# A blockwise attention stage: packed copies for queries and keys, and the causal mask of the maximum pass moved to TensorE

## The chip, the cores and the metric

The kernel runs on one core of a Trainium2 chip. The metric is the device time of one execution in microseconds (us), the median of several runs; lower is better.

## The reference

The program is six residual blocks over x of 4 x 1024 x 128: expert FFN, attention, expert FFN (layer 0), then expert FFN, gated attention, expert FFN (layer 1). Only the first attention is touched by the change. With 16 heads of 8 dimensions it computes, for a layer-normed x:

```python
qkv = x @ w_in.T + b_in
q, k, v = to_heads(split(qkv))              # 4 x 16 x 1024 x 8
scores = einsum('bhqd,bhkd->bhqk', q * (1 / sqrt(8)), k)
scores = scores + where(tril, 0, -inf)      # causal
attn = softmax(scores)
out = einsum('bhqk,bhkd->bhqd', attn, v) @ w_out.T + b_out
```

The FFN blocks before and after and the gated attention are the same in both kernels.

## The kernel before

`phase_attention` (line 643) works in 16 sections, n = 0 to 15: four batches of 1024 tokens, and four groups of four heads in each. `order()` (line 675) gives each piece of work a due time in units of one section, and `walk` lets every engine go through its pieces in that one order. The engines are tied together by semaphores, and each engine does its pieces strictly in that order.

**Projection** (`proj`, twice per w, once per half of 512 tokens). TensorE leaves q (w = 0) or k (w = 1) in a bank; ScalarE writes a rounded high part into `high` (line 980), VectorE the rest into `low` (line 1102). A product then needs three terms: high by high, low by high and high by low.

**Copies on the Sync queue.** `queries(n)` fills slot n % 3 of `q_st`: three DMAs of 32 partitions by 1024 (high, low, high; line 1056) and one DMA of eight rows of `k_pad` that sets the rows for the maxima (line 1058). `keys(n, h)` fills half h of slot n % 2 of `k_pad`: for each of four heads, three DMAs of 8 partitions by 512 (high, high, low; line 1070), so twelve. `k_pad` is zero outside the rows of its own head. `keys(n, h)` first waits (line 1065) until section n-2 is scored up to unit 8 (h = 0) or to its end (h = 1), since it writes over its slot.

**Maximum pass** (`max`, due from n-1.26 to n-0.30). For each of four heads, nine banks (`MAXB`) hold the scores of all 8 query tiles against the keys that they can see: 12 products a head, line 886. Before the first product of a section TensorE waits for its queries and the first half of its keys. VectorE takes the maximum of each bank (`peak`, lines 1109 to 1118): a block that touches the diagonal by a `tensor_tensor_reduce` that adds the tile `mask` (line 1114), each other block by a `tensor_reduce` (line 1116). The three banks of the ring `SMALL` are shared with transposes and projections. `neg` combines the maxima (lines 1123 to 1130, due n-0.3), `maxt` (due n-0.25) transposes them on TensorE (line 895), ScalarE copies them out (line 986), and Sync puts them into `q_st` (line 1045), so that the products of the next pass come out with the maximum taken off.

**Score and value passes** (due n to n+1). Twelve units in a section, for each two pairs of heads: TensorE scores (line 905), ScalarE takes the exponential (line 994), GpSimd clears the part above the diagonal (line 1028), TensorE multiplies by the values (line 924, fp32), due two units later. `oevac` and `ot` (lines 1001, 933) follow at the end of a half.

The due times put these pieces in this order on TensorE around the start of the maximum pass of section n+1 (with the section that they belong to): score (n-1, unit 7, pair 1), max (n, last), score (n-1, 8, 0), pv (n-1, 6), max (n+1, first), maxt (n), score (n-1, 8, 1).

Of the kernel before, what the change touches and what calls it, by code (L numbers as in the profile page):

```python
# [6 lines left out]
F32 = mybir.dt.float32  # L7
# [6 lines left out]
P = 128  # L14
# [628 lines left out]
def phase_attention(nc, k, a):  # L643
# [25 lines left out]
    def order():  # L669
# [13 lines left out]
        for n in range(SECTIONS):  # L683
# [43 lines left out]
    with ExitStack() as ctx:  # L727
# [8 lines left out]
        b_in, bo, ones = sb("b_in", [P, 3]), sb("bo", [P, D]), sb("ones", [2, S])  # L736
        mask = sb("mask", [P, G])
        st, mv, veps, rstd = sb("st", [P, NB, 6]), sb("mv", [P, NB, 2]), sb("veps", [P, NB]), sb("rstd", [P, NB])
        xn = sb("xn", [P, NB, D])
        xn_h, xn_l = sb("xn_h", [P, S], F32R), sb("xn_l", [P, S], F32R)  # L740
        high, low = sb("high", [P, 2, S], F32R), sb("low", [P, 2, S], F32R)
        q_st, k_pad = sb("q_st", [P, 3, S], F32R), sb("k_pad", [P, 2, HG, S], F32R)
        v_t, v_aug = sb("v_t", [P, S]), sb("v_aug", [P, 2, NB, H * VH + 32 - VH])
        mx, nm, mst = sb("mx", [P, HG, HALF * NB]), sb("nm", [P, HG * NB]), sb("mst", [P, 2 * HG * NB])
# [11 lines left out]
        with nc.Block() as block:  # L756
            @block.sync
            def _(sp):
# [7 lines left out]
                for p in range(2):  # L766
                    for j in range(HG):
                        rows = slice(MROW + j, MROW + j + HG + 1, HG)
                        sp.dma_start(k_pad[rows, p, j, :].bitcast(F32), ones[:]).then_inc(ones_in, 16)
# [11 lines left out]
            def _(pool):  # L781
                pool.memset(ones[:], 1.0)
# [13 lines left out]
            def _(dve):  # L796
                dve.memset(q_st[:].bitcast(F32), 0.0)
                dve.memset(mask[:, 0:G - P], 0.0)
                dve.tensor_copy(mask[:, G - P:G], k.const("causal"))
# [9 lines left out]
        xh_done, qk_high = sem("xh_done"), sem("qk_high")  # L809
# [34 lines left out]
        def _(pe):  # L844
# [31 lines left out]
            def peak(n, j, i):  # L876
                bank, full = fill(pe, "max", n, j, i)
                at = 0
                if i == 0 and j == 0:
                    pe.wait_ge(q_in[n % 3], 16 * 4 * (n // 3 + 1))  # L880
                    pe.wait_ge(k_in[n % 2][0], 16 * 3 * HG * (n // 2 + 1))
                if i == HALF1 and j == 0:
                    pe.wait_ge(k_in[n % 2][1], 16 * 3 * HG * (n // 2 + 1))
# [71 lines left out]
        def _(act):  # L955
# [16 lines left out]
            def proj(b, w, h):  # L972
                bank, _ = content(act, "proj", b, w, h)
                cut = slice(h * G, (h + 1) * G)
                if b > 0 and w == 0:
                    for p in range(3):
                        act.wait_ge(q_in[p], 16 * 4 * len(range(p, HG * b, 3)))
# [716 lines left out]
```

## Time and profile before

| what | value |
|---|---|
| median of 3 runs | 2221.54 us (2219.11 to 2221.6) |
| the profiled execution | 2220.21 us |
| its span, first to last instruction | 2218.5 us |
| TensorE busy | 1768.8 us, 80% |
| VectorE busy | 1464.7 us, 66% |
| ScalarE busy | 960.4 us, 43% |
| GpSimd busy | 706.0 us, 32% |
| mean granted TensorE clock | 0.903 |

The attention lies between 262 and 1022 us of the span. A share of the whole span is a mean over six phases; what the change can do has to be read inside that stretch. Each line of a profile names the source line (L886), the engine (PE is TensorE, PEld its weight loads, DVE VectorE, ACT ScalarE, POOL GpSimd, SPq the Sync queue's DMA issues), the tiles written and read, and what ended an idle time before the instruction.

### The profile page before, as it was taken

The page shows a single profiled execution, that of the slowest core. Times are in us where ns is not written, and L with a number is a line of the kernel's source. Part 1 is how long each engine was busy: PE and PEld are TensorE (multiplying, and loading weights), DVE is VectorE, ACT ScalarE, POOL GpSimd, SP SyncE. Part 2 cuts the span into 40 slices and gives each one's busy share as a digit, 9 for nine tenths or more (in the row PEclk, how much of TensorE's full clock was granted, in tenths as well). Part 3 has the DMA queues.
Part 4 walks back from the last instruction along what each step waited for, and adds up shares of the span by engine and source line. Part 5 has one row for each costly group of instructions (what it writes and reads, how often), then busy time and mean ns, then how long its engine had stood idle before and what let it go on. Part 6 is the DMA issues. An engine that isn't in the chain of part 4 may idle for free. (4 is left out here: it accounts for less than half of the span.)

```text
span 2218.5 us, 28736 instructions
## 1 busy us (share of the span) xinstructions
PE 1768.8 (80%) x8768; PEld 1267.4 (57%) x8768; DVE 1464.7 (66%) x4307; ACT 960.4 (43%) x1579; POOL 706.0 (32%) x641
## 2 busy tenths in 40 slices
PE   4988668787888688886888769999925666899997
PEld 3666434444444344543666557777824555677776
DVE  4788657665667566753878557767637775677774
ACT  2444314454455355554444335545512222455554
POOL 1444511201211211111444325555511110455554
PEclk8999858998999889997999979999967888999998
DMA  3000011100010001100000110000010000000001
GB/s 85 1 1 0 8 27 20 24 17 19 18 24 18 19 17 22 21 9 0 1 1 0 35 33 1 1 1 0 1 31 1 0 0 1 1 1 1 0 0 38
DMA packets 27250, 27.75 MB, mean 13 GB/s; under 512 B 9609, under 2 KB 19682, under 8 KB 27122
## 3 DMA queue, kind: packets, MB, share of 16 engines
q1 hardware_dynamic: 24418, 24.09, 4.8%
q10 hardware_dynamic: 2576, 2.10, 0.3%
q8 instruction: 58, 0.95, 0.2%
q14 instruction: 70, 0.57, 0.1%
q0 software_dynamic: 128, 0.03, 0.1%
HBM read 10.41 MB, written 2.10 MB: 6 GB/s over the span
## 5 line engine op out<-in xcount | busy, mean ns | idle before, releaser
L994 ACT ACTIVATE att_probs<-banks 128x1024 f32<-128x1024 f32 (+3 forms) x384 | 303.7, 812 | 200.9 <-PE banks L905 198.5
L886 PE MATMUL banks<-att_k_pad,att_q_st 128*128 128x512 f32 (+3 forms) x768 | 254.7, 418 | 135.7 <-DMA att_k_pad<-att_low 121.5
L1114 DVE CUSTOM_DVE_ANT_0 banks<-banks,att_mask 128x128 f32<-128x128 f32 (+3 forms) x512 | 235.7, 522 | 174.9 <-PE banks L886 174.4
L886 PEld LDWEIGHTS banks<-att_k_pad,att_q_st 128*128 128x128 f32 x768 | 139.0, 207 | 262.4 <-issue 206.6
L1028 POOL TENSOR_SCALAR_AFFINE_SELECT att_probs<-att_probs 128x512 f32<-128x512 f32 x128 | 81.6, 637 | 563.8 <-ACT att_probs L994 563.8
L905 PE MATMUL banks<-att_q_st,att_k_pad 128*128 128x512 f32 (+3 forms) x768 | 218.0, 369 | 0.6 <-ACT att_probs L994 0.4
L462 POOL TENSOR_TENSOR ffn1a_hid_l<-ffn1a_hid,ffn1a_hid_h 128x512 fp32r<-128x512 f32 x128 | 165.2, 1293 | 130.8 <-ACT ffn1a_hid_h L418 130.8
L462 POOL TENSOR_TENSOR ffn1b_hid_l<-ffn1b_hid,ffn1b_hid_h 128x512 fp32r<-128x512 f32 x128 | 165.3, 1294 | 129.3 <-ACT ffn1b_hid_h L418 129.3
L1116 DVE TENSOR_REDUCE att_mx<-banks 128x1 f32<-128x512 f32 x256 | 161.5, 683 | 36.0 <-PE banks L886 35.8
L924 PE MATMUL banks<-att_probs,att_v_aug 128*32 128x512 f32 (+3 forms) x1536 | 172.2, 521 | 0.6 <-POOL att_probs L1028 0.5
L905 PEld LDWEIGHTS banks<-att_q_st,att_k_pad 128*128 128x128 f32 x768 | 143.0, 200 | 39.1 <-ACT att_probs L994 20.0
L601 DVE TENSOR_TENSOR ffn1a_scl<-ffn1a_sil,banks 128x512 f32<-128x512 f32 x128 | 88.0, 687 | 84.3 <-PE banks L317 42.4
L601 DVE TENSOR_TENSOR ffn1b_scl<-ffn1b_sil,banks 128x512 f32<-128x512 f32 x128 | 88.0, 688 | 81.3 <-PE banks L317 40.7
L410 ACT ACTIVATE ffn1a_sil<-banks 128x512 f32<-128x512 f32 x128 | 76.7, 599 | 115.2 <-PE banks L312 112.4
L410 ACT ACTIVATE ffn1b_sil<-banks 128x512 f32<-128x512 f32 x128 | 76.7, 599 | 114.3 <-PE banks L312 111.5
L462 POOL TENSOR_TENSOR ffn0b_hid_l<-ffn0b_hid,ffn0b_hid_h 128x512 fp32r<-128x512 f32 x72 | 92.4, 1288 | 103.3 <-ACT ffn0b_hid_h L418 103.3
L462 POOL TENSOR_TENSOR ffn0a_hid_l<-ffn0a_hid,ffn0a_hid_h 128x512 fp32r<-128x512 f32 x72 | 92.4, 1287 | 102.9 <-ACT ffn0a_hid_h L418 102.9
L609 DVE TENSOR_TENSOR ffn1a_hid<-ffn1a_scl,banks 128x512 f32<-128x512 f32 x128 | 87.9, 687 | 7.6 <-POOL ffn1a_hid_l L462 2.4
L609 DVE TENSOR_TENSOR ffn1b_hid<-ffn1b_scl,banks 128x512 f32<-128x512 f32 x128 | 87.9, 687 | 6.3 <-POOL ffn1b_hid_l L462 1.8
L418 ACT ACTIVATE ffn1a_hid_h<-ffn1a_hid 128x512 fp32r<-128x512 f32 x128 | 79.9, 624 | 8.0 <-DVE ffn1a_hid L609 8.0
L418 ACT ACTIVATE ffn1b_hid_h<-ffn1b_hid 128x512 fp32r<-128x512 f32 x128 | 79.8, 624 | 4.5 <-DVE ffn1b_hid L609 4.5
L601 DVE TENSOR_TENSOR ffn0b_scl<-ffn0b_sil,banks 128x512 f32<-128x512 f32 x72 | 49.3, 685 | 40.8 <-PE banks L322 39.9
(439 smaller groups left out, 4302.4 us busy)
## 6 DMA issues: line engine op xcount, KB each, us to landing
att_q_st<-att_high SPq DMA_DIRECT2D x32, 128.0 KB
att_k_pad<-att_high SPq DMA_DIRECT2D x256, 16.0 KB
att_q_st<-att_low SPq DMA_DIRECT2D x16, 128.0 KB
att_k_pad<-att_low SPq DMA_DIRECT2D x128, 16.0 KB
out_dram<-x SPq DMA_DIRECT2D x1, 2048.0 KB, 8.7
raw<-in_L_ffn_w_dram SPq DMA_DIRECT2D x3, 512.0 KB, 13.7
raw<-in_L_ffn_w_down_dram SPq DMA_DIRECT2D x1, 1024.0 KB, 11.4
sel_raw<-in_consts_dram SPq DMA_DIRECT2D x1, 576.0 KB, 4.4
```

Source lines behind the costliest of these rows:

```text
L410: act.activation(sil[:, n, :], gate_ps[:, n, :], ACT.Silu).then_inc(silu_done, 1)
L418: act.activation(hid_h[:, n, :], hid[:, n, :], ACT.Copy).then_inc(high_cut, 1)
L462: pool.tensor_tensor(hid_l[:, n, :], hid[:, n, :], hid_h[:, n, :].bitcast(F32), ALU.subtract)\
L601: dve.tensor_tensor(scl[:, n, :], sil[:, n, :], comb_ps[:, comb_bank(q, c), :], ALU.mult).then_inc(scaled, 1)
L609: dve.tensor_tensor(hid[:, n, :], scl[:, n, :], up_ps[:, n, :], ALU.mult).then_inc(hidden, 1)
L886: mm = pe.matmul(bank[:, at:at + width], q_st[:, n % 3, t * P:(t + 1) * P], k_pad[:, n % 2, j, c * G:c * G + width], start=True, stop=True ...
L905: mm = pe.matmul(score_ps[:, pair, h, 0:c], k_pad[:, n % 2, 2 * pair + h, kb * P:(kb + 1) * P], q_st[:, n % 3, (qg + 1) * G - c:(qg + 1) * ...
L924: mm = pe.matmul(o_ps[32 * j:32 * j + 32, G - c:G], v_aug[:, b % 2, kb, at:at + 32], probs[:, unit % NPROB, j, 0:c], start=kb == 0, stop=k ...
L994: act.activation(probs[:, unit % NPROB, 2 * pair:2 * pair + 2, 0:c], score_ps[:, pair, :, 0:c], ACT.Exp, scale=SCALE).then_inc(exped, 1)
L1028: pool.affine_select(now, now, pattern=[[0, HG], [1, P]], base=0, channel_multiplier=-1, compare_op=ALU.is_ge, fill=0.0).then_inc(masked, 1)
L1114: ins = dve.tensor_tensor_reduce(now, now, mask[:, G - width:G], 1.0, -3e38, ALU.add, ALU.max, best)
L1116: ins = dve.tensor_reduce(best, now, AX.X, ALU.max)
```

## The change

1. `high` and `low` become one tile `parts` of 128 x 2 x 3 x 1024. Part 0 is the high part (ScalarE), one further part is the low part (VectorE, `LOW`), and the third is a copy of the high part (`AGAIN`), made by GpSimd in a new piece `proj`: a `tensor_copy` of 128 x 512 for each projection, 16 in all. A semaphore `qk_again` tells Sync of it.
2. `queries(n)` issues one DMA of 32 partitions by three rows into 96 partitions, and the one for the maxima rows as before: two in place of four. `keys(n, h)` issues one DMA a head, 8 partitions by three rows into 24 partitions: four in place of twelve. The rows of `q_st` and `k_pad` change places accordingly.
3. The diagonal blocks are masked on TensorE: after the product of such a block a second one, the identity by the causal tile, both bfloat16 and 128 columns wide, adds the mask into the last 128 columns. There are 8 such blocks a head and section, 512 in all.
4. VectorE reads each bank with one `tensor_reduce` (36 a section; four groups of 128, two of 256 or one of 512) into a wider `mx`, and `neg` reads this with another pattern.
5. The maximum pass is due from n-1.22 to n-0.29 in place of n-1.26 to n-0.30. With this `maxt(n)` and score (n-1, 8, 1) come before the first product of section n+1.
6. The tile `ones` lies in `xn`, the tile `mask` is gone, and `ident_b` and `causal_b` are made at the start of the phase.

```diff
+    LOW, AGAIN = (1, 2), (2, 1)
+    MAXTO = (slice(20, 21), slice(8, 9), slice(25, 26), slice(15, 16), slice(28, 29), slice(3, 7),
+             slice(29, 30), slice(11, 15), slice(16, 25, 8))
+    PARTS = (1, 1, 1, 1, 1, 4, 1, 4, 2)
...
-                    put(n - 1.26 + 0.96 * (i * HG + j) / (len(MAXB) * HG), "max", n, j, i)
+                    put(n - 1.22 + 0.93 * (i * HG + j) / (len(MAXB) * HG), "max", n, j, i)
...
-                    pe.wait_ge(q_in[n % 3], 16 * 4 * (n // 3 + 1))
-                    pe.wait_ge(k_in[n % 2][0], 16 * 3 * HG * (n // 2 + 1))
+                    pe.wait_ge(q_in[n % 3], 16 * 2 * (n // 3 + 1))
+                    pe.wait_ge(k_in[n % 2][0], 16 * HG * (n // 2 + 1))
...
+                    diag = c == t // TG
                     mm = pe.matmul(bank[:, at:at + width], q_st[:, n % 3, t * P:(t + 1) * P],
-                                   k_pad[:, n % 2, j, c * G:c * G + width], start=True, stop=True,
+                                   k_pad[:, n % 2, j, c * G:c * G + width], start=True, stop=not diag,
                                    skip_group_check=True)
                     at += width
+                    if diag:
+                        mm = pe.matmul(bank[:, at - P:at], ident_b[:], causal_b[:], start=False, stop=True,
+                                       skip_group_check=True)
...
+            def proj(b, w, h):
+                step = 4 * b + 2 * w + h
+                cut = slice(h * G, (h + 1) * G)
+                pool.wait_ge(qk_high, step + 1)
+                pool.tensor_copy(parts[:, w, AGAIN[w], cut], parts[:, w, 0, cut].bitcast(F32)).then_inc(qk_again, 1)
...
+                sp.wait_ge(qk_again, 4 * b + 2)
...
-                for r, part in enumerate((high, low, high)):
-                    sp.dma_start(q_st[32 * r:32 * r + 32, n % 3, :].bitcast(F32), part[own, 0, :].bitcast(F32))\
-                      .then_inc(q_in[n % 3], 16)
+                sp.dma_start(q_st[0:MROW, n % 3, :].bitcast(F32), parts[hg * 32:hg * 32 + 32, 0, :, :].bitcast(F32))\
                   .then_inc(q_in[n % 3], 16)
...
+                sp.wait_ge(qk_again, 4 * b + 3 + h)
                 for j in range(HG):
                     own = slice((hg * HG + j) * DH, (hg * HG + j) * DH + DH)
-                    for r, part in enumerate((high, high, low)):
-                        sp.dma_start(k_pad[32 * r + j * DH:32 * r + (j + 1) * DH, n % 2, j, cut].bitcast(F32),
-                                     part[own, 1, cut].bitcast(F32)).then_inc(k_in[n % 2][h], 16)
+                    sp.dma_start(k_pad[3 * DH * j:3 * DH * (j + 1), n % 2, j, cut].bitcast(F32),
+                                 parts[own, 1, :, cut].bitcast(F32)).then_inc(k_in[n % 2][h], 16)
...
-                for t, c in MAXB[i]:
-                    width = width_of(t, c)
-                    now, best = bank[:, at:at + width], mx[:, j, 2 * t + c:2 * t + c + 1]
-                    if c == t // TG:
-                        ins = dve.tensor_tensor_reduce(now, now, mask[:, G - width:G], 1.0, -3e38, ALU.add, ALU.max, best)
-                    else:
-                        ins = dve.tensor_reduce(best, now, AX.X, ALU.max)
-                    at += width
-                ins.then_inc(empty, 1)
+                dve.tensor_reduce(mx[:, j, MAXTO[i]], bank.rearrange("p (n c) -> p n c", n=PARTS[i]), AX.X, ALU.max)\
+                   .then_inc(empty, 1)
```

## Rows read from the trace of the kernel before

**Rows 1.** The page: busy time of each engine over the span.

```profile
PE 1768.8 (80%) x8768; PEld 1267.4 (57%) x8768; DVE 1464.7 (66%) x4307; ACT 960.4 (43%) x1579; POOL 706.0 (32%) x641
```

**Rows 2.** Busy time by stretch: stretch, length, engines (instructions), clock, DMA share, GB/s.

```profile
344.00:1016.00 672.00, 542.79 (x3299) 309.37 (x3298) 420.47 (x1380) 338.08 (x463) 111.60 (x160) 0.91 0.09 19
```

**Rows 3.** Who waited for whom, 300 to 1035 us: total, times, longest.

```profile
PE banks L886 <- DMA att_k_pad<-att_low: 121.5, 15, 10.8
PEld banks L886 <- DVE att_mx L1114: 27.9, 64, 2.9
PE banks L886 <- DVE att_mx L1114: 9.1, 10, 2.5
```

**Rows 4.** Timeline around one such wait: start, us, engine, line, operation, idle before.

```profile
584.59 0.63 PE L905 MATMUL banks<-att_q_st,att_k_pad 128*128 128x512 f32 x2
...
585.30 1.31 SPq L1070 DMA_DIRECT2D att_k_pad<-att_high  x2
...
585.85 1.07 PE L924 MATMUL banks<-att_probs,att_v_aug 128*32 128x512 f32 x8
...
592.65 0.62 SPq L1070 DMA_DIRECT2D att_k_pad<-att_low  x1
...
594.76 0.77 PE L886 MATMUL banks<-att_k_pad,att_q_st 128*128 128x512 f32 x1 [7.84 <-DMA att_k_pad<-att_low]
```

**Rows 5.** Timeline: the first and the last of the 14 such waits.

```profile
370.39 0.77 PE L886 MATMUL banks<-att_k_pad,att_q_st 128*128 128x512 f32 x1 [7.84 <-DMA att_k_pad<-att_low]
...
952.74 0.77 PE L886 MATMUL banks<-att_k_pad,att_q_st 128*128 128x512 f32 x1 [7.84 <-DMA att_k_pad<-att_low]
```

**Rows 6.** DMA issues by source line: count, ns min/median/max, first and last start.

```profile
L1070 SPq DMA_DIRECT2D att_k_pad<-att_low x128: 624/625/642, 300.4 to 969.9; - x128
L1056 SPq DMA_DIRECT2D att_q_st<-att_low x16: 584/591/602, 297.1 to 930.3; - x16
L142 SPq DMA_DIRECT2D raw<-in_L_ffn_w_dram x2: 433/560/686, 1.7 to 2.8; - x2
```

**Rows 7.** Timeline of the last section, where no keys are awaited.

```profile
986.98 0.27 PE L895 MATMUL banks<-pack,att_mst 128*64 128x128 f32 x1 [1.23 <-DVE att_mst L1130]
```

**Rows 8.** Busy time by stretch, right after two of the waits (columns as Rows 2).

```profile
594.70:598.40 3.70, 3.64 (x12) 2.44 (x16) 2.10 (x6) 1.51 (x3) 0.64 (x1) 0.50 0.03 9
598.40:602.10 3.70, 3.70 (x25) 1.72 (x18) 1.97 (x6) 1.90 (x3) 0.64 (x1) 0.99 0.00 0
644.40:649.60 5.20, 5.09 (x16) 2.42 (x16) 2.16 (x6) 2.11 (x3) 0.64 (x1) 0.50 0.04 11
```

**Rows 9.** Timeline: products in a row on TensorE.

```profile
566.94 0.33 PE L905 MATMUL banks<-att_q_st,att_k_pad 128*128 128x128 f32 x2
567.99 0.66 PE L933 MATMUL banks<-pack,att_o_sb 128*128 128x128 f32 x4
```

**Rows 10.** Groups of instructions by form, 300 to 1035 us: busy, mean ns, idle before.

```profile
L886 PE MATMUL banks<-att_k_pad,att_q_st 128*128 128x128 f32 x128 | 36.0, 281 | 8.6 <-DVE att_mx L1114 7.5 <-DVE att_low L1102 0.6
```

**Rows 11.** Groups of instructions on the page: busy, mean ns, idle before.

```profile
L1114 DVE CUSTOM_DVE_ANT_0 banks<-banks,att_mask 128x128 f32<-128x128 f32 (+3 forms) x512 | 235.7, 522 | 174.9 <-PE banks L886 174.4
L1028 POOL TENSOR_SCALAR_AFFINE_SELECT att_probs<-att_probs 128x512 f32<-128x512 f32 x128 | 81.6, 637 | 563.8 <-ACT att_probs L994 563.8
L462 POOL TENSOR_TENSOR ffn1a_hid_l<-ffn1a_hid,ffn1a_hid_h 128x512 fp32r<-128x512 f32 x128 | 165.2, 1293 | 130.8 <-ACT ffn1a_hid_h L418 130.8
L1116 DVE TENSOR_REDUCE att_mx<-banks 128x1 f32<-128x512 f32 x256 | 161.5, 683 | 36.0 <-PE banks L886 35.8
```

**Rows 12.** Timeline of the phase's start.

```profile
294.85 2.09 ACT L980 ACTIVATE att_high<-banks,att_b_in 128x512 fp32r<-128x512 f32 x3 [0.59 <-PE banks L858]
...
296.49 0.56 SPq L1056 DMA_DIRECT2D att_q_st<-att_high  x1
...
299.08 1.32 SPq L1070 DMA_DIRECT2D att_k_pad<-att_high  x2
...
308.55 1.62 PE L886 MATMUL banks<-att_k_pad,att_q_st 128*128 128x512 f32 x3 [10.75 <-DMA att_k_pad<-att_low]
```

More of the change, by code:

```diff
@@ L735, in phase_attention @@
         wo_t = sb("wo_t", [P, P])
-        b_in, bo, ones = sb("b_in", [P, 3]), sb("bo", [P, D]), sb("ones", [2, S])
-        mask = sb("mask", [P, G])
+        b_in, bo = sb("b_in", [P, 3]), sb("bo", [P, D])
+        ident_b, causal_b = sb("ident_b", [P, P], BF16), sb("causal_b", [P, P], BF16)
         st, mv, veps, rstd = sb("st", [P, NB, 6]), sb("mv", [P, NB, 2]), sb("veps", [P, NB]), sb("rstd", [P, NB])
         xn = sb("xn", [P, NB, D])
+        ones = xn[0:2, :, :].rearrange("p t d -> p (t d)")
         xn_h, xn_l = sb("xn_h", [P, S], F32R), sb("xn_l", [P, S], F32R)
-        high, low = sb("high", [P, 2, S], F32R), sb("low", [P, 2, S], F32R)
+        parts = sb("parts", [P, 2, 3, S], F32R)
         q_st, k_pad = sb("q_st", [P, 3, S], F32R), sb("k_pad", [P, 2, HG, S], F32R)
         v_t, v_aug = sb("v_t", [P, S]), sb("v_aug", [P, 2, NB, H * VH + 32 - VH])
-        mx, nm, mst = sb("mx", [P, HG, HALF * NB]), sb("nm", [P, HG * NB]), sb("mst", [P, 2 * HG * NB])
+        mx, nm, mst = sb("mx", [P, HG, 4 * NB]), sb("nm", [P, HG * NB]), sb("mst", [P, 2 * HG * NB])
         m_t = sb("m_t", [2 * HG * NB, P])
@@ L768, in _ @@
                         rows = slice(MROW + j, MROW + j + HG + 1, HG)
-                        sp.dma_start(k_pad[rows, p, j, :].bitcast(F32), ones[:]).then_inc(ones_in, 16)
+                        sp.dma_start(k_pad[rows, p, j, :].bitcast(F32), ones).then_inc(ones_in, 16)
                 sp.wait_ge(w_in, 16 * 6)
@@ L781, in _ @@
             def _(pool):
-                pool.memset(ones[:], 1.0)
+                pool.memset(ones, 1.0)
                 pool.memset(k_pad[:].bitcast(F32), 0.0).then_inc(zeroed, 1)
@@ L797, in _ @@
                 dve.memset(q_st[:].bitcast(F32), 0.0)
-                dve.memset(mask[:, 0:G - P], 0.0)
-                dve.tensor_copy(mask[:, G - P:G], k.const("causal"))
+                dve.tensor_copy(ident_b[:], k.ident)
+                dve.tensor_copy(causal_b[:], k.const("causal"))
                 dve.wait_ge(high_done, 1)
@@ L976, in proj @@
                     for p in range(3):
-                        act.wait_ge(q_in[p], 16 * 4 * len(range(p, HG * b, 3)))
+                        act.wait_ge(q_in[p], 16 * 2 * len(range(p, HG * b, 3)))
                     for p in range(2):
-                        act.wait_ge(k_in[p][h], 16 * 3 * HG * (HG * b // 2))
-                act.activation(high[:, w, cut], bank, ACT.Identity, bias=b_in[:, w:w + 1]).then_inc(qk_high, 1)
+                        act.wait_ge(k_in[p][h], 16 * HG * (HG * b // 2))
+                act.activation(parts[:, w, 0, cut], bank, ACT.Identity, bias=b_in[:, w:w + 1]).then_inc(qk_high, 1)
             def maxt(n):
@@ L1035, in wo @@
                 pool.tensor_tensor(xs, xs, ypos[:].rearrange("p t d -> p (t d)"), ALU.add).then_inc(x_added, 1)
-            walk(dict(norm=norm, mask=mask, wo=wo))
+            walk(dict(norm=norm, proj=proj, mask=mask, wo=wo))
         @block.sync
@@ L1101, in proj @@
                 dve.wait_ge(qk_high, 4 * b + 2 * w + h + 1)
-                dve.scalar_tensor_tensor(low[:, w, cut], bank, b_in[:, w:w + 1], high[:, w, cut].bitcast(F32),
+                dve.scalar_tensor_tensor(parts[:, w, LOW[w], cut], bank, b_in[:, w:w + 1], parts[:, w, 0, cut].bitcast(F32),
                                          ALU.add, ALU.subtract).then_inc(empty, 1)
@@ L1122, in neg @@
                     drained(dve, "max", n, j, len(MAXB) - 1)
-                dve.tensor_reduce(nm[:], mx[:].rearrange("p j (t c) -> p (j t) c", c=HALF), AX.X, ALU.max, negate=True)\
+                dve.tensor_reduce(nm[:].rearrange("p (j q o) -> p j o q", q=NB // 2, o=2),
+                                  mx[:].rearrange("p j (o q s) -> p j o q s", o=2, s=4), AX.X, ALU.max, negate=True)\
                    .then_inc(neg_steps, 1)
```

9 lines of the change are left out of this document (4 added, 5 removed).

## The prediction

> **What bounds the kernel now.** I read the page first, only to see that no engine is full over the whole span [rows 1]; six phases are mixed there. So I took the stretch from the first score to near the last, 344 to 1016 us [rows 2]. TensorE is busy 542.8 of its 672 us, VectorE 420.5, ScalarE 338.1. Then the list of waits in the phase [rows 3]. TensorE waits for the keys' DMAs 15 times, 121.5 us in all; the next entries, waits of its weight loads and products for VectorE, come to 37.0 us together (27.9 + 9.1). One of the 15 is the start (10.75 us, [rows 12]), the other 14 lie one in each section from n = 2 on, the first and the last 7.84 us long [rows 5] and the rest no shorter (121.5 - 10.75 = 110.75 for all 14); 14 x 7.84 = 109.8 us is what I count. Without these, 672 - 109.8 = 562 us are left, and TensorE is busy in 543 of them, 97%. (A busy time with waiting weight loads in it says too much, but nothing else is near.) So in the attention TensorE sets the pace, and its largest hole is the wait for keys.
>
> The timeline shows why the hole is there [rows 4]. The score product that starts at 584.59 frees the slot, and Sync issues the first key DMA at 585.30. Twelve follow, the last at 592.65: (592.65 - 585.30) / 11 = 0.668 us apart. The last has landed 2.1 us after its issue, at 594.76. TensorE is through with its value products at 585.85 + 1.07 = 586.92 and stands until 594.76. Landing is thus 9.46 us after the first issue, of which 7.35 us are the issuing of eleven further DMAs.
>
> **Part 1, key DMAs: four in place of twelve.** The last issue is 3 x 0.668 = 2.0 us after the first. An issue takes 0.62 us for 8 rows of 2 KB and 0.59 us for 32 rows of 4 KB [rows 6], so it doesn't go by rows; a three-dimensional load of 1024 rows of 512 B was issued in 0.43 to 0.69 us. I take 0.67. Each DMA now carries three times the bytes, for which I add 0.5 us (an estimate: twelve DMAs of one row an engine moved inside 0.67 us intervals, so three rows can't need more than 2 us, and the DMA engines are 9% busy here [rows 2]). Landing: 2.0 + 2.1 + 0.5 = 4.6 us after the first issue, 589.9 on the clock of [rows 4]; bounds 4.1 and 6.1.
>
> The Trainium skill, "DMA: Bandwidth & Descriptors", section "Why a DMA increments its semaphore by 16 and not by 1", says that the number of DMA engines is the largest up to 16 that divides the slowest dimension of both sides; 8 and 24 partitions would give eight engines as before, three rows on each. By that the packing wins issue time but no width, and the 0.5 us are needed; with 16 engines they would be about half, 14 x 0.25 = 3.5 us less in the sum.
>
> **Part 2, the new order.** Between the freeing of the slot and the first product of the new section TensorE now has one more bank of the section before (about 0.5 us with its mask products), `maxt` (0.3 to 0.4) and one more score pair (0.63 less overlap, 0.45). `maxt` waits for VectorE to finish the maxima and for `neg`. Today that is hidden behind the keys, but the last section, which awaits no keys, shows it: 1.23 us [rows 7]. So TensorE would come to the keys at 586.92 + 0.5 + 1.23 + 0.4 + 0.45 = 589.5, against 589.9: 0.4 us left. New waits: 1.23 + 0.4 = 1.7 us in a section, 14 x 1.7 = **24 us back of 109.8** (bounds 1.2 and 3.5 us a section). Everything on TensorE is queued behind the wait at `maxt`: the scores, and with them ScalarE, which has slack.
>
> **Part 3, the clock.** After each wait the granted clock is 0.50, that is 1.2 GHz, for 3.7 to 5.2 us, and then 0.99, 2.4 GHz [rows 8]. In that time TensorE does 12 products in 3.7 us against 25 in the next 3.7 (not the same mix). Before it, TensorE had done nothing for 7.84 us. With waits of 1.2 and 0.4 us I expect most drops to vanish; half of 4.4 us is 2.2, of which I take 1.5 since not all of that stretch is bound by TensorE: **-21 us** (bounds 0 and -29). The Trainium skill, "TensorE: Matmul & The Clock Gate", section "HAM oscillation — how this bites in real kernels", also describes waits for DMA that bring the clock down each time; the trace agrees with 0.50 behind these waits, and whether 1.2 us of idling suffices no row here says.
>
> **Part 4, the start.** The first key DMA is issued at 299.08 and the first product starts at 308.55 [rows 12]. The query copies now also wait for two GpSimd copies of 128x512, not in the trace; GpSimd's nearest are 0.64 us (one operand, in place) and 1.29 us (two operands, fp32r out) [rows 11], I take 1. The second high part is ready at about 295.55 (294.85 plus a third of 2.09), so queries start at 296.6 rather than 296.49, two DMAs later keys start at 297.9, held by no copy (third copy about 297.4), and land at 302.5 to 303: **-5.6 us**. In the later batches the same copies are due 0.15 to 0.3 of a section ahead of the queries, and GpSimd is 17% busy (111.6 of 672, [rows 2]): nothing. Where it delays a mask by a copy of 1 us, the value products come two units later.
>
> **Part 5, 512 more products on TensorE.** None of them is in the trace. 32 of them belong to section 0, where VectorE's maxima set the pace alone; 480 lie on the bound engine. Lower bound: two 128-column products in a row end 0.33 us after the first starts, one alone takes 0.27, so the second adds 0.06 us [rows 9]. Upper, with each product behind a load: four in 0.66 us, (0.66 - 0.27) / 3 = 0.13 us. The load of the identity can go on under the 128 to 512 columns ahead of it, but the load that follows has only 128 columns to hide under. I take 0.09, between them: 480 x 0.09 = **+43 us** (29 to 62). The far end is a product whose whole 0.28 us are exposed [rows 10]; that is a rival below.
>
> The Trainium skill, "TensorE: Matmul & The Clock Gate", section "Back-to-back issue gap", gives N / 2.4 + 2.5 ns, 56 ns for 128 columns, and its section on fast weight load lets bfloat16 weights of 128 columns load faster than fp32. By that the sum of this part would be 27 us, at the lower bound from the rows; no run so far shows a bfloat16 load here.
>
> **Part 6, VectorE.** For one head and section it has 8 masked blocks at a mean of 0.522 us and 4 reductions at 0.683 [rows 11], 6.9 us, part of it overlapped; nine reductions of 512 columns are 9 x 0.683 = 6.1. It gets up to 0.8 us a head faster, 3 us a section, and it isn't the bound: 0, with up to -15 us if 15 of the 37.0 us of waits for it [rows 3] go. The new `neg` reads 128 x 128 in place of 128 x 64, about 0.1 us more in each chain; nothing. The two setup copies take the place of one memset and one copy: nothing.
>
> **Sum**, against the profiled 2220.2 us (1.3 us below the median of 2221.5): -109.8 + 24 - 21 - 5.6 + 43 = -69, so 2151 us.
>
> **The rivals.**
>
> - A, *the mask products cost next to nothing*, hidden in the gaps that the ring's waits leave anyway [rows 3], and VectorE's relief counts. For it: two 128-column products 0.06 us apart [rows 9]. Against: 97% busy. Saves 30 of the 43 and 10 of the waits: about 2111 us.
> - B, *a leftover wait keeps the clock down*: the keys land 1.5 us later than I say and each section still idles 3.2 us in pieces, with the clock at 0.50 behind it. 2151 + 14 x 1.5 + 21 = 2193 us. For it: three rows on each engine, and the wait at `maxt` is one that the old order hid.
> - C, on the other side, *the mask products drain the array*: a change from fp32r to bfloat16 and back lets each of the 480 be exposed with its full 0.28 us [rows 10], 134 us. The time is 2220.2 - 112.4 + 134 = 2242, slower. It decides from 112.4 / 480 = 0.234 us a product on. Against it: the products with fp32 weights and with fp32r weights follow each other in this trace without such a price ([rows 4], 584.59 to 585.85).
> - D, *the packing wins nothing*: a DMA's issue goes by its rows after all, 2 us for each, so that the keys land as late as now. What is gained is the 1.3 us of work moved ahead of the wait, 14 x 1.3 = 18, and 43 are paid: 2245 us, slower. Against: [rows 6].
>
> **How the numbers follow.** The forecast gets 0.55, A 0.20, B 0.15, C 0.07, D 0.03. The predicted time is 2151. Its own range is 2130 to 2175 by the bounds of parts 1, 3 and 5. To hold the time 8 times in 10 the range takes in A and B, 2108 to 2200; left out are C, D and the edges. About 0.2% (4.4 us) is what a measurement of this kernel can tell from no change. Faster by more than that are the forecast, A and B with 0.89, 0.02 is for between, slower are C and D with 0.09.
>
> **What would show it.** Part 1: four issues of about 0.65 us apart at the line of the keys, and a wait of under 1 us there in place of 7.84. Part 2: a wait of 1 to 1.5 us at `maxt` for `neg`, in every section. Part 3: the clock at 0.99 where `maxt` and the first maxima of a section run. Part 4: the first product of section 0 near 303 us. Part 5: starts of the bfloat16 product and the next one 0.06 to 0.13 us apart; the time from section to section down from 44.8 us ((952.74 - 370.39) / 13, [rows 5]) to some 40. What would make the prediction wrong is a price of the mask product outside 0.06 to 0.13, or an issue of a key DMA of over 1 us.

## The result and the profile after

The changed kernel takes 2141.85 us (median of 4 runs, 2139.88 to 2143.93), the one before 2220.32 beside it. The ratio is 0.9651, with a 95% interval of 0.9633 to 0.9668: 3.5% faster, 78 us. The profiled execution has a span of 2138.1 us against 2218.5, 80.4 less. All of it lies in the attention: from the first transposes of its weights to the last of its products it takes 944.99 - 269.73 = 675.3 us, and took 1022.56 - 266.70 = 755.9. (The phase starts 3 us later in this execution and the phases behind it are 3 us shorter; such shifts between executions bound what single profiles can tell.)

First who waits for whom in the changed kernel, from 300 to 950 us (total, times, longest), which answers [rows 3]. L892 is the product of the maximum pass, L897 its mask product, L904 the transpose of the maxima, L1123 the reduction, L1084 the key DMA.

```profile
PE banks L892 <- DMA att_k_pad<-att_parts: 27.5, 15, 5.6
PEld banks L892 <- DVE att_mx L1123: 16.5, 35, 1.7
PE banks L904 <- DVE att_mst L1137: 7.0, 16, 2.0
PE banks L892 <- DVE att_mx L1123: 2.2, 3, 0.8
```

The waits for keys are 27.5 us in place of 121.5: one of 5.6 at the start and 14 of some 1.56. The waits for VectorE at the banks fell from 45.7 us (37.0 behind the masked blocks, [rows 3], and 8.7 behind the plain reductions) to 18.7, and the transpose of the maxima waits 7.0 us in all, 2.0 of them in section 0.

The timeline around the same place as in [rows 4], one section of the changed kernel:

```profile
552.22 0.39 PE L914 MATMUL banks<-att_q_st,att_k_pad 128*128 128x512 f32 x1
...
552.68 2.84 SPq L1084 DMA_DIRECT2D att_k_pad<-att_parts  x4
...
553.99 1.07 PE L933 MATMUL banks<-att_probs,att_v_aug 128*32 128x512 f32 x8
...
555.39 0.27 PE L904 MATMUL banks<-pack,att_mst 128*64 128x128 f32 x1 [0.33 <-DVE att_mst L1137]
...
555.41 0.71 PE L914 MATMUL banks<-att_q_st,att_k_pad 128*128 128x512 f32 x2
...
557.61 0.47 PE L892 MATMUL banks<-att_k_pad,att_q_st 128*128 128x512 f32 x1 [1.48 <-DMA att_k_pad<-att_parts]
```

Four issues begin at 552.68 and end 2.84 us later, so with 0.67 us for one they follow each other every 0.72 us ((2.84 - 0.67) / 3). The keys are there at 557.61, 4.93 us after the first issue, where it was 9.46. TensorE now does the transpose and one more score pair before it asks for them.

The stretches, as in [rows 2] and [rows 8]: first the kernel before over 344 to 930 us, then the changed one over the same.

```profile
344.00:930.00 586.00, 466.68 (x2813) 270.08 (x2813) 379.02 (x1226) 284.59 (x392) 99.09 (x140) 0.90 0.10 20
```

```profile
344.00:930.00 586.00, 550.80 (x3698) 311.27 (x3694) 387.66 (x717) 332.58 (x450) 115.26 (x167) 0.99 0.12 21
```

TensorE is busy 94% of the time in place of 80%, and the granted clock went from 0.90 to 0.99. The issues and the two new kinds of instruction, as in [rows 6] and [rows 11] (count, ns min/median/max, first and last start; the last line is a group of the page):

```profile
L1084 SPq DMA_DIRECT2D att_k_pad<-att_parts x128: 670/673/1212, 300.7 to 885.4; - x128
L1037 POOL CAST att_parts<-att_parts x16: 609/612/617, 297.1 to 743.7; 128x512 fp32r<-128x512 f32 x16
L897 PEld LDWEIGHTS banks<-att_causal_b,att_ident_b x512: 94/96/149, 306.7 to 907.3; 128*128 128x128 bf16 x171
...
L1123 DVE TENSOR_REDUCE att_mx<-banks 128x1 f32<-128x512 f32 (+2 forms) x576 | 367.9, 685 | 146.8 <-PE banks L897 111.1
```

### The profile page after: what moved, and what is told of

It reads as the page before. It is cut to its first block and busy times, and to the rows that moved or that the text cites. A ratio compares the mean times of both kernels' runs of the same rounds, so it can differ in the third digit from the quotient of the medians.

```text
span 2138.1 us, 28801 instructions
## 1 busy us (share of the span) xinstructions
PE 1788.4 (84%) x9280; PEld 1275.3 (60%) x9280; DVE 1434.0 (67%) x3603; ACT 963.9 (45%) x1579; POOL 714.6 (33%) x657
## 5 line engine op out<-in xcount | busy, mean ns | idle before, releaser
L1123 DVE TENSOR_REDUCE att_mx<-banks 128x1 f32<-128x512 f32 (+2 forms) x576 | 367.9, 685 | 146.8 <-PE banks L897 111.1
L892 PE MATMUL banks<-att_k_pad,att_q_st 128*128 128x512 f32 (+3 forms) x768 | 268.9, 416 | 31.9 <-DMA att_k_pad<-att_parts 27.5
L892 PEld LDWEIGHTS banks<-att_k_pad,att_q_st 128*128 128x128 f32 x768 | 148.8, 200 | 128.7 <-issue 105.7
L933 PE MATMUL banks<-att_probs,att_v_aug 128*32 128x512 f32 (+3 forms) x1536 | 166.6, 506 | 0.6 <-POOL att_probs L1043 0.5
L914 PEld LDWEIGHTS banks<-att_q_st,att_k_pad 128*128 128x128 f32 x768 | 130.7, 193 | 22.0 <-ACT att_probs L1003 11.3
L897 PE MATMUL banks<-att_causal_b,att_ident_b 128*128 128x128 bf16 x512 | 118.2, 235 | 0.0
L897 PEld LDWEIGHTS banks<-att_causal_b,att_ident_b 128*128 128x128 bf16 x512 | 50.6, 99 | 47.3 <-issue 25.2
## 6 DMA issues: line engine op xcount, KB each, us to landing
raw<-in_L_ffn_w_dram SPq DMA_DIRECT2D x3, 512.0 KB, 13.7
```

Source lines behind the costliest of these rows:

```text
L897: mm = pe.matmul(bank[:, at - P:at], ident_b[:], causal_b[:], start=False, stop=True, skip_group_check=True)
L914: mm = pe.matmul(score_ps[:, pair, h, 0:c], k_pad[:, n % 2, 2 * pair + h, kb * P:(kb + 1) * P], q_st[:, n % 3, (qg + 1) * G - c:(qg + 1) * ...
L933: mm = pe.matmul(o_ps[32 * j:32 * j + 32, G - c:G], v_aug[:, b % 2, kb, at:at + 32], probs[:, unit % NPROB, j, 0:c], start=kb == 0, stop=k ...
L1123: dve.tensor_reduce(mx[:, j, MAXTO[i]], bank.rearrange("p (n c) -> p n c", n=PARTS[i]), AX.X, ALU.max)\
```

## The experiments

The change has three parts that can be taken one at a time: P, the packed DMAs; D, the new due times; M, the mask on TensorE with the single reduction on VectorE. My theory was that TensorE sets the pace, that P and D remove its wait, and that M costs it time. Each kernel was timed beside the kernel before; runs of different sets were on different chips, so I compare ratios. Times are medians in us. Multiplied by 2220 a ratio step of 0.001 is 2.2 us.

| parts | kernel | time | ratio (95% interval) |
|---|---|---|---|
| P | packed DMAs alone | 2152.5 | 0.9694 (0.9678 to 0.9711) |
| M | mask alone | 2245.4 | 1.0112 (1.0095 to 1.0129) |
| D | due times alone | 2211.0 | 0.9960 (0.9947 to 0.9972) |
| P M | changed kernel, old due times | 2175.3 | 0.9794 (0.9763 to 0.9824) |
| P D | changed kernel, mask on VectorE | 2113.2 | 0.9514 (0.9498 to 0.9530) |
| M D | changed kernel, twelve key DMAs | 2230.3 | 1.0054 (1.0037 to 1.0071) |
| P M D | the changed kernel | 2141.9 | 0.9651 (0.9633 to 0.9668) |

### The mask products left out

```diff
-                    if diag:
-                        mm = pe.matmul(bank[:, at - P:at], ident_b[:], causal_b[:], start=False, stop=True,
-                                       skip_group_check=True)
```

> The changed kernel with its 512 mask products left out: the maximum pass then takes maxima over the unmasked diagonal blocks (that part of the computation is changed). Everything else stays. Theory P (TensorE sets the pace, a mask product costs 0.09 us): 480 x 0.09 = 43 us less, of which some 4 come back because TensorE reaches the keys earlier: 2142 - 43 + 4 = 2103 us. Rival H (the mask products lie in gaps that are there anyway): within 5 us of 2142. Rival X (a bfloat16 product between fp32r ones costs its own 0.04 us and about 0.085 us of gap ahead of it, 0.125 in all): 2142 - 60 + 4 = 2086 us.

Measured: 2104.4 us, ratio 0.9472 (0.9452 to 0.9492). 37.5 us less by the medians, 39.7 by the ratios, so 0.078 to 0.083 us for each of 480 products. That is theory P's cost: the products are not hidden. Its 4 us that come back are not seen, though. Without the products TensorE waits less for the keys (23.4 us in place of 27.5) and more for the maxima (13.7 in place of 7.0) and for VectorE's banks (30.4 in place of 18.7), 14 us more in all. The 0.08 us is thus what is left after those waits: if they all count, the products themselves took up to (37.5 + 14) / 480 = 0.11 us each (an estimate from the two lists of waits), and a quarter of that lay in waits that are there anyway.

### Packed DMAs alone

The edit: from the changed kernel, the mask and the maxima on VectorE as before (its tile `mask` back, no mask products) and the due times set back.

```diff
-                    put(n - 1.22 + 0.93 * (i * HG + j) / (len(MAXB) * HG), "max", n, j, i)
+                    put(n - 1.26 + 0.96 * (i * HG + j) / (len(MAXB) * HG), "max", n, j, i)
...
-                    if diag:
-                        mm = pe.matmul(bank[:, at - P:at], ident_b[:], causal_b[:], start=False, stop=True,
...
+                    if c == t // TG:
+                        ins = dve.tensor_tensor_reduce(now, now, mask[:, G - width:G], 1.0, -3e38, ALU.add, ALU.max, best)
+                    else:
+                        ins = dve.tensor_reduce(best, now, AX.X, ALU.max)
```

> Packed DMAs alone: query and key copies as in the changed kernel, but the mask added by VectorE as before, the old due times (n-1.26 to n-0.30), no mask products. Theory P: the keys land 4.93 us after the first issue as measured in the changed kernel, TensorE reaches them 1.62 us after it as before, so the wait is 3.3 us in place of 7.84: 14 x 4.5 = 63 us less, 5 at the start, and 5 to 15 of the clock: 2220 - 63 - 5 - 10 = 2142 us, as fast as the full change. Rival V (VectorE's relief carries the gain, the DMAs little): above 2190 us.

Measured: 2152.5 us, 67 less than before, far from rival V but 10 more than I expected. Its wait line (300 us to the end of the phase) and its stretch over 344 to 930 us:

```profile
PE banks L892 <- DMA att_k_pad<-att_parts: 53.4, 15, 5.3
```

```profile
344.00:930.00 586.00, 520.01 (x3149) 296.98 (x3149) 415.50 (x1369) 320.99 (x438) 114.02 (x164) 0.94 0.12 21
```

The waits are what I said, (53.4 - 5.3) / 14 = 3.4 us each. What is missing is the 10 us of the clock: the waits shrank by 121.5 - 53.4 = 68.1 us and the span by 2218.5 - 2150.5 = 68.0, so next to nothing came back beside them. The mean clock is 0.94 in place of 0.90 all the same, because a mean over a stretch counts the waits themselves. In the kernel before, the clock falls while TensorE still waits (first line, behind its last product at 586.92); here it falls near the end of the wait or behind it, and the products pay as before (second line, right behind a wait of 3.31 us):

```profile
592.00:593.00 1.00, 0.00 (x0) 0.00 (x0) 0.00 (x0) 0.00 (x0) 0.00 (x0) 0.50 0.12 23
```

```profile
607.36:613.38 6.02, 6.02 (x18) 3.20 (x19) 2.23 (x7) 2.11 (x3) 0.64 (x1) 0.50 0.04 10
```

Added up from the clock and the products in the traces, from 344 us to the end of the attention, TensorE worked at 0.50 for 68.7 us in the kernel before, for 66.9 here, and for 13.7 in the changed kernel.

### The mask alone

The edit is that of the change (its items 3 and 4) in the kernel before, with twelve key DMAs and the old due times.

```diff
+                    if diag:
+                        mm = pe.matmul(bank[:, at - P:at], ident_b[:], causal_b[:], start=False, stop=True,
+                                       skip_group_check=True)
...
-                        ins = dve.tensor_tensor_reduce(now, now, mask[:, G - width:G], 1.0, -3e38, ALU.add, ALU.max, best)
+                dve.tensor_reduce(mx[:, j, MAXTO[i]], bank.rearrange("p (n c) -> p n c", n=PARTS[i]), AX.X, ALU.max)\
```

> The mask alone: the kernel before with the mask as bfloat16 products on TensorE and one reduction a bank on VectorE, old due times, twelve key DMAs. Theory P: 480 x 0.09 = 43 us more, 0 to 10 back from waits for VectorE: 2253 to 2263 us, slower than before. Rival V (VectorE's relief carries the gain): 2180 us or less. Rival X (0.125 us a product): 2270 to 2280 us.

Measured: 2245.4 us, 25 more than before. Rival V falls: relieving VectorE doesn't carry the gain. It is less than my 33 to 43 though; the waits of weight loads for VectorE's maxima, 36.6 us in the lists of the kernel before (27.9 of them in [rows 3]), are 14.6 here:

```profile
PEld banks L890 <- DVE att_mx L1116: 14.6, 35, 1.6
```

### The old due times under the full change

```diff
-                    put(n - 1.22 + 0.93 * (i * HG + j) / (len(MAXB) * HG), "max", n, j, i)
+                    put(n - 1.26 + 0.96 * (i * HG + j) / (len(MAXB) * HG), "max", n, j, i)
```

> The changed kernel with the old due times of the maximum pass (n-1.26 and 0.96). Theory P: TensorE reaches the keys about 1.5 us earlier (one bank, the transpose of the maxima and one score pair come behind the wait again), so the wait is 3.3 us in place of 1.5 and the wait for the maxima goes: 14 x 1.5 = 21 us more, and up to 15 if the clock drops behind a wait of 3.3 us: 2163 to 2178 us. Rival O (the order moves nothing, idle time only changes its place): within 4 us of 2142.

Measured: 2175.3 us, 33 more. Rival O falls. Its waits for keys are 50.0 us in place of 27.5, those for the maxima 1.8 in place of 7.0 and those for VectorE's banks 21.2 in place of 18.7: 20 us of the 35 by which the spans differ (2173.4 - 2138.1). The other 15 go with the clock, at 0.96 in place of 0.99 over 344 to 950 us; TensorE works at 0.50 for 43.8 us, not 13.7:

```profile
PE banks L892 <- DMA att_k_pad<-att_parts: 50.0, 15, 5.6
```

```profile
344.00:950.00 606.00, 552.06 (x3620) 314.65 (x3620) 387.35 (x714) 321.91 (x437) 113.65 (x163) 0.96 0.11 20
```

### Packed DMAs and new due times, mask on VectorE

The edit is that of the packed kernel above, without its first hunk.

> Packed DMAs and the new due times, but the mask added by VectorE as before: the changed kernel without its part on TensorE. Theory S (the parts add, VectorE isn't the bound): the packed kernel with old due times took 2152.5, and the new due times gave 2175.3 - 2141.9 = 33 us with the mask on TensorE, so 2119 us, faster than the full change; the kernel without any mask product and with the short reductions, 2104.4, is the floor. Rival D (the new due times need VectorE relieved: the transpose of the maxima now stands ahead of the keys and waits for VectorE's longer chain): the wait there grows to 2 us a section, 2140 us or more.

Measured: 2113.2 us, ratio 0.9514 (0.9498 to 0.9530). This is faster than the full change by 0.0137, 30 us. The waits of its phase:

```profile
PEld banks L892 <- DVE att_mx L1125: 36.1, 95, 2.0
PE banks L901 <- DVE att_mst L1141: 21.2, 16, 2.4
PE banks L892 <- DMA att_k_pad<-att_parts: 15.0, 15, 5.6
```

Rival D is right in its mechanism and wrong in its weight. Without the relief the transpose of the maxima does wait, 2.4 us in section 0 and 1.2 to 1.6 in each other one (21.2 over 16), but in that time the keys land, so their waits shrink from 27.5 to 15.0.

### Each mask product twice

```diff
                     if diag:
+                        pe.matmul(bank[:, at - P:at], ident_b[:], causal_b[:], start=False, stop=False,
+                                  skip_group_check=True)
                         mm = pe.matmul(bank[:, at - P:at], ident_b[:], causal_b[:], start=False, stop=True,
```

> The changed kernel with each mask product issued twice in a row (the mask is then added twice, which leaves masked places masked). Theory P (a mask product costs its columns wherever it stands; leaving 480 out saved 37.5 us, 0.078 each): 2142 + 37 = 2179 us. Rival L (what costs is the fp32r weight load that follows the 128 columns and can't hide under them, once for each pair): only the product itself is added, 0.04 to 0.06 us, 2161 to 2171 us. Rival H (hidden): 2142 us.

Measured: 2163.8 us, ratio 0.9735 (0.9719 to 0.9751): 22 us more for 480 products by the medians, 19 by the ratios, 0.04 to 0.05 each. The first one costs 0.08. That is the range of theory L. The timeline (L899 is the second of the two):

```profile
568.58 0.47 PE L892 MATMUL banks<-att_k_pad,att_q_st 128*128 128x512 f32 x1 [1.37 <-DMA att_k_pad<-att_parts]
568.89 0.23 PE L897 MATMUL banks<-att_causal_b,att_ident_b 128*128 128x128 bf16 x1
568.96 0.22 PE L899 MATMUL banks<-att_causal_b,att_ident_b 128*128 128x128 bf16 x1
```

The doubled product starts 0.07 us behind the first.

### The mask in fp32r

```diff
-        ident_b, causal_b = sb("ident_b", [P, P], BF16), sb("causal_b", [P, P], BF16)
+        ident_b, causal_b = sb("ident_b", [P, P], F32R), sb("causal_b", [P, P], F32R)
```

> The changed kernel with the identity and the causal tile in fp32r in place of bfloat16. Rival C of the prediction in its small form (it is the change of type that costs: the pair of a 256-column product and its mask product takes 0.246 us in the trace of the changed kernel, where two 256-column products alone are 0.117 apart): up to 0.04 us less for each of 480, 2122 us. Theory L (the cost is the next weight load, which hasn't enough columns to hide under): no change, 2137 to 2147 us, or up to 0.03 us more for each where the identity's own load is longer, 2157 us.

Measured: 2145.9 us, ratio 0.9658 (0.9642 to 0.9674), no difference from 0.9651. In the sum neither the change of type nor the bfloat16 decides, although the weight load of the identity is recorded at 191 ns here and at 96 in bfloat16:

```profile
L897 PEld LDWEIGHTS banks<-att_causal_b,att_ident_b x512: 187/191/338, 306.5 to 909.8; 128*128 128x128 f32 x171
```

But the equal times are a balance of two small differences. Behind a 256-column product, the product and its mask take 0.23 us in fp32r (the first lines) and 0.25 us in bfloat16 (the second):

```profile
554.50 0.33 PE L892 MATMUL banks<-att_k_pad,att_q_st 128*128 128x256 f32 x1
554.67 0.22 PE L897 MATMUL banks<-att_causal_b,att_ident_b 128*128 128x128 f32 x1
554.73 0.33 PE L892 MATMUL banks<-att_k_pad,att_q_st 128*128 128x256 f32 x1
```

```profile
552.61 0.36 PE L892 MATMUL banks<-att_k_pad,att_q_st 128*128 128x256 f32 x1
552.82 0.23 PE L897 MATMUL banks<-att_causal_b,att_ident_b 128*128 128x128 bf16 x1
552.86 0.36 PE L892 MATMUL banks<-att_k_pad,att_q_st 128*128 128x256 f32 x1
```

Behind a 128-column and a 384-column product, the two pairs together take 0.51 us in fp32r (551.48 to 551.99 in that trace) and 0.49 in bfloat16 (540.44 to 540.93). So rival C in its small form isn't excluded: what it would save at the wide products can be what the longer load of an fp32r identity costs at the narrow ones. No run separates the two.

### A semaphore for the first head's keys

```diff
+        k_first = [sem(f"k_first{p}") for p in range(2)]
...
-                    pe.wait_ge(k_in[n % 2][0], 16 * HG * (n // 2 + 1))
+                    pe.wait_ge(k_first[n % 2], 16 * (n // 2 + 1))
+                if i == 0 and j == 1:
+                    pe.wait_ge(k_in[n % 2][0], 16 * (HG - 1) * (n // 2 + 1))
...
-                                 parts[own, 1, :, cut].bitcast(F32)).then_inc(k_in[n % 2][h], 16)
+                                 parts[own, 1, :, cut].bitcast(F32)).then_inc(k_first[n % 2] if h == j == 0 else k_in[n % 2][h], 16)
```

> The changed kernel with a semaphore of its own for the first head's key DMA, so that TensorE waits for one DMA before the first product and for the other three only before the second head's. Theory P: the wait of 1.5 us goes and some 0.3 to 0.5 us come back one bank later: 14 x 1.1 = 15 us less, and the four short half clocks go: 2124 to 2130 us. Rival M (the wait moves whole to the second head): within 4 us of 2142.

Measured: 2130.5 us, ratio 0.9582 (0.9565 to 0.9599), but with runs from 2127.5 to 2140.1 us, of which the profiled one is the slowest. In its trace the waits only shrank from 27.5 to 22.9 us:

```profile
PE banks L895 <- DMA att_k_pad<-att_parts: 22.9, 16, 3.6
```

Each section still has a wait of 1.2 to 1.9 us, now one product later, so most of it goes to the second head, as rival M has it. The waits are 4.6 us shorter in this trace, yet its span is that of the changed kernel (2138.4 against 2138.1), so the phases outside made up for it in this execution. The medians show 11 us of gain and the ratios 15, which is theory P's number without its mechanism. Where the rest of the gain comes from stays open.

### The due times alone

```diff
-                    put(n - 1.26 + 0.96 * (i * HG + j) / (len(MAXB) * HG), "max", n, j, i)
+                    put(n - 1.22 + 0.93 * (i * HG + j) / (len(MAXB) * HG), "max", n, j, i)
```

> The kernel before with the new due times alone: twelve key DMAs, mask on VectorE. Theory P (the keys land 9.46 us after their first issue whatever TensorE does; the new order puts some 1.5 us of work, a wait for the maxima among it, ahead of that): 14 x 1.0 to 1.5 = 14 to 21 us less, 2200 to 2207 us. Rival A (the parts add as if independent: the new due times are worth 33 to 39 us anywhere): 2181 to 2187 us. Rival O (nothing until the keys are quick): 2220 us.

Measured: 2211.0 us, 9 less than before; the interval (0.9947 to 0.9972) leaves no doubt of a small gain, less than theory P's 14 to 21. The waits for keys fall by 38 us, but 18.4 come back at the transpose of the maxima (21.2 in place of 2.8 in the sections without keys, [rows 7]), and 8 more at the banks that VectorE frees (53.6 us in place of 45.7; the second line is their largest part, 27.9 in [rows 3]). That leaves 12 us by the waits, and the spans differ by 9.4:

```profile
PE banks L886 <- DMA att_k_pad<-att_low: 83.6, 15, 10.8
...
PEld banks L886 <- DVE att_mx L1114: 36.2, 95, 2.0
...
PE banks L895 <- DVE att_mst L1130: 21.2, 16, 2.4
```

Rival A falls: the due times are worth 9 us with slow keys and 40 us with quick ones (0.9694 against 0.9514).

### Twelve key DMAs under the full change

```diff
-                    sp.dma_start(k_pad[3 * DH * j:3 * DH * (j + 1), n % 2, j, cut].bitcast(F32),
-                                 parts[own, 1, :, cut].bitcast(F32)).then_inc(k_in[n % 2][h], 16)
+                    for r in range(3):
+                        sp.dma_start(k_pad[3 * DH * j + r:3 * DH * (j + 1):3, n % 2, j, cut].bitcast(F32),
+                                     parts[own, 1, r, cut].bitcast(F32)).then_inc(k_in[n % 2][h], 16)
```

The counts that TensorE and ScalarE wait for are three times as large.

> The changed kernel with its key copies issued as twelve DMAs again, into the new rows; queries packed, mask on TensorE, new due times. Theory P: the keys land at about 9.3 us after the first issue in place of 4.93, so each of 14 waits is 4.4 us longer, 62 us, and the clock falls behind each, 10 to 20 us: 2214 to 2224 us. Rival Q (part of the gain comes from the packed queries or from the smaller load on the Sync queue elsewhere): 2190 us or less.

Measured: 2230.3 us, ratio 1.0054 (1.0037 to 1.0071). It is slower than the kernel before, and 6 us above theory P's range; packing the keys is worth 88 us here. This pair also measures the clock, since both have the same products in the same order. The twelve-DMA kernel's waits and its stretch:

```profile
PE banks L892 <- DMA att_k_pad<-att_parts: 94.2, 15, 10.1
```

```profile
330.00:980.00 650.00, 550.64 (x3488) 309.26 (x3487) 388.03 (x714) 312.27 (x423) 111.01 (x160) 0.91 0.10 20
```

The spans differ by 2225.1 - 2138.1 = 87.0 us, the waits for keys by 94.2 - 27.5 = 66.7. The waits for the maxima and for VectorE's banks are the same within 1 us. The other 20.3 us go with a clock of 0.91 in place of 0.99: TensorE works at 0.50 for 69.6 us in place of 13.7.

### Two kernels on top of the faster combination

Packed DMAs, new due times, mask on VectorE and the first head's semaphore; then the same with the maximum pass due later:

```diff
-                    put(n - 1.22 + 0.93 * (i * HG + j) / (len(MAXB) * HG), "max", n, j, i)
+                    put(n - 1.19 + 0.90 * (i * HG + j) / (len(MAXB) * HG), "max", n, j, i)
```

> Packed DMAs, new due times, mask on VectorE, and the semaphore of its own for the first head's keys. Theory P: the kernel without that semaphore took 2113.2 and its trace has 9.4 us of waits for keys behind the start, most of which go: 2104 to 2110 us. Rival M (the wait only goes to the second head or to the transpose of the maxima): 2110 to 2116 us.

Measured: 2110.2 us, ratio 0.9504 (0.9489 to 0.9520), not told apart from the 0.9514 without the semaphore; it lies at the edge of both theories. The waits for keys are 11.1 us in place of 15.0.

> As the kernel with packed DMAs, new due times, mask on VectorE and the first head's semaphore, but the maximum pass due from n-1.19 over 0.90. Theory P (the remaining waits are keys that are a little late): the last of them go, 2100 to 2108 us. Rival D (the maxima end no earlier, so the wait at the transpose of the maxima stays, and a denser pass makes TensorE wait for VectorE's reductions more): equal to or slower than the kernel with n-1.22 and 0.93.

Measured: 2105.9 us, ratio 0.9482 (0.9466 to 0.9498). It is the fastest kernel here that does the whole computation, 1.7% below the changed kernel; its step from 0.9504 is inside the intervals. Both theories name a part of what its list shows: the keys' waits are gone but for the start, as theory P has it. The wait at the transpose of the maxima stays, and the waits for VectorE's banks grow from 53.3 to 64.2 us, as rival D has it.

```profile
PE banks L904 <- DVE att_mst L1145: 21.2, 16, 2.4
...
PE banks L895 <- DMA att_k_pad<-att_parts: 4.8, 2, 3.5
```

## Why the prediction was right, point by point

The forecast was 2151 us and the measured time is 2141.9; the mechanism and the side were right, and most of the difference of 9 us has a name. The time from section to section fell from 44.8 to 39.2 us ((874.03 - 364.04) / 13, from the first products behind the waits), where I had said some 40.

| term | forecast | measured | from |
|---|---|---|---|
| waits for keys and maxima, 14 sections | -109.8 + 24 = -86 | -110.8 + 21.9 + 4.2 = -85 | keys 110.8 to 21.9, transposes 2.8 to 7.0 |
| clock | -21 | -20 | twelve against four key DMAs (waits of 6.0 and 1.5 us) |
| start | -5.6 | -5.1 | first wait, 10.75 to 5.64 |
| 480 mask products | +43 | +38 to +40 | kernel without them |
| VectorE | 0 | -9 | with and without its mask: 2113.2 - 2104.4 |
| sum | -69 | -80 | spans: -80.4 |

The first and the third row are read from waits, the others from pairs of kernels, which also differ by 1 to 3 us in the waits of the first row. That the rows add up to the difference of the spans holds within some 3 us.

**Part 1, the DMAs.** The keys landed at 4.93 us, against 4.6 with bounds of 4.1 and 6.1. I had used 0.67 us as the time from issue to issue; one issue takes that, and they follow every 0.72 us, so the last begins 2.17 us after the first and not 2.0. Three times the bytes cost a little more than my 0.5 us: 4.93 - 2.17 - 2.1 = 0.7. Rival D (an issue goes by its rows) is out.

**Part 2, the order.** This part is right in its sum and wrong in how it is shared out. The wait at the transpose of the maxima came out at 0.33 us in the section shown, not 1.23, so my sign of 1 to 1.5 us there failed, and so did that of under 1 us at the keys. The row I took it from had VectorE's longer chain; with the mask on VectorE it is 1.2 us in every section, with the mask on TensorE it is nearly gone. What I gained there went to the keys, 1.5 us in place of 0.4, so the sum of both, 1.8, is the 1.7 of the forecast: since the keys land when they land, a shorter wait ahead makes a longer one behind.

**Part 3, the clock.** The size is right and the kernel with twelve DMAs gives it by a measurement. That 1.5 us of waiting doesn't bring the clock down was open; it does in only 4 of the 14 sections (0.99 over the stretch). Waits of 3.4 us still bring it down in every section, and the step from 7.84 to 3.4 us gave next to nothing back beside the waits. So the 20 us hang on the waits being as short as the packing and the new order make them together.

**Part 4, the start.** TensorE stands 5.64 us ahead of the first product in place of 10.75. The copy on GpSimd takes 0.61 us, where I took 1. My sign was that they begin near 303 us; they begin at 306.1, 3.0 us of which is that the whole phase starts later in this execution.

**Part 5, the mask products.** 0.078 to 0.083 us against 0.09. Rivals A and C are out: the products are neither free nor exposed with their full 0.28 us. A has a point all the same, since up to a quarter of what they take lies in waits that shrink in turn. The 27 us that the prediction worked out from the formula for a product by itself are too low. That a further product costs 0.04 to 0.05 us and the first of a pair 0.08 fits a next weight load with too few columns to hide under; the load as the cause is argued from these two prices, it isn't shown by a row, and the fp32r kernel doesn't decide it.

**Part 6, VectorE.** This is the term that was mis-sized most, 0 against -9 us. I kept the 15 us as a bound and put nothing in the sum, because VectorE isn't the bound. It isn't, but TensorE waits for its banks a little at a time. The relief by itself shortens these waits from 53.8 to 30.4 us (from the kernel with packed DMAs and new due times to the one without mask products), and 9 us of that show in the time. From the kernel before to the changed one they shrink from 45.7 to 18.7 us, but there the mask products slow TensorE down as well. In the forecast I counted only the 37.0.

What the prediction didn't ask is whether each part pays. M costs 22 us with the old due times, 25 alone and 30 with the new ones. P alone brings 68 and P with D 108; the full change brings 78 because it hands 30 back.

## What to carry to other kernels

Work that moves from an engine with slack to the engine that sets the pace costs time there, here 0.08 us for each of 480 short bfloat16 products and more than VectorE's relief gave back: take each part of a change by itself before keeping all of them. Where many small DMAs feed one wait, what counts is the number of issues ahead of the last one, so pack them, and then set the consumer's due time to the new landing, for due times that did little before were worth several times as much here once the transfer was quick (40 us in place of 9). A wait cut short on TensorE can also give back the clock behind it, here a quarter of what the waits themselves were; but only the last step did so, from some 3.4 us down to 1.5, and the larger one from 7.8 to 3.4 gave next to nothing. The mean clock of a stretch doesn't tell this, since the waits are in it; look at the clock where the engine works.

## What the runs showed of the hardware

- The issue of a DMA on the Sync queue takes 0.67 us for 24 rows from three-dimensional source patterns, 0.62 for 8 rows and 0.59 for 32, so it doesn't go by rows.
- The granted clock over the attention was 0.99 with waits of 1.5 us, 0.94 to 0.96 with 3.1 to 3.4 us, and 0.90 to 0.91 with 6 to 8 us, each once a section of 39 to 46 us. 1.0 and 0.5 are the two levels, 2.4 and 1.2 GHz. The time for which TensorE worked at 0.5 was 14 us, 44 to 67 us and 69 to 70 us in these three groups.
- The 128-column mask products cost the same in sum with fp32r as with bfloat16 operands (2145.9 and 2141.9 us), though the recorded weight load is twice as long (191 against 96 ns).
- The two small copies that make the mask tiles are recorded with 6.9 us each at the start of the phase, beside a memset of `k_pad` of 6.9 us on GpSimd:

```profile
265.17 6.91 POOL L788 MEMSET att_k_pad<- 128x8192 f32 x1
...
267.53 6.91 DVE L803 CAST att_ident_b<-pack 128x128 bf16<-128x128 f32 x1
267.61 6.89 DVE L804 CAST att_causal_b<-pack 128x128 bf16<-128x128 f32 x1
...
272.04 2.31 POOL L789 MEMSET att_v_aug<- 128x2672 f32 x1
```

Both begin while GpSimd's first memset runs and end at 274.4 to 274.5, when GpSimd's second memset is through (274.35). VectorE's next instruction starts at 274.43. The kernel before shows the same with its copy of the mask (6.50 us), so no difference between the two kernels comes of it. The Trainium skill, "SBUF — State Buffer", section "SBUF: two separate sides", says that GpSimd and some VectorE operations on SBUF hold one pair of ports in turn, each for its whole instruction, and the other waits. The trace agrees, as far as these rows can tell: the copies get through only when both memsets are done.
